# Sorting two row tiles in one instruction a stage, with ScalarE's copies of the idle ends made twice a merge

## What is computed

```python
def _L0_conv_ref(x):                       # x is normalised over its channels
    x3 = x.reshape(B, M, F)                # M = 4096 positions, F = 256
    corr = jnp.einsum('bmf,bnf->bmn', x3, x3) / F
    s = -jnp.sort(-corr, axis=-1)          # every row of 4096 sorted, largest first
    ranks = jnp.round(jnp.linspace(1.0, M - 1, NB_POOLS)).astype(jnp.int32)
    pooled = jnp.take(s, ranks, axis=-1)   # 256 of the 4096
    return pooled.reshape(B, H, W, NB_POOLS)
...
x = x + _L0_conv_ref(_ln_c(x))
t = _to_tokens(x)
t = t + _L0_ffn_ref(_ln_t(t), ...)         # experts, routed by attention over 1048576 edges
```

## Time and profile before

| | |
|---|---|
| median of three runs | 31163.97 us (31161.8 to 31172.99) |
| span of the profiled execution | 31832.6 us |
| `pool_rows`, first to last DVE instruction of the full stages | 4662 to 29096 us |
| DVE busy | 28357.2 us, 89% |
| PE busy | 25816.8 us, 81% |
| ACT busy | 22199.6 us, 70% |
| POOL busy | 15519.9 us, 49% |

### The profile page before, as it was taken

One profiled execution on the slowest core, in us unless ns is written; L12 is line 12 of the kernel. 1 busy time (PEld: TensorE's weight loads), 2 busy tenths in 40 slices (PEclk: granted clock), 3 DMA queues, 4 the chain that ended last, 5 costly groups with the idle time before them and its releaser, 6 DMA issues. The chain is left out here.

```text
span 31832.6 us, 519908 instructions
## 1 busy us (share of the span) xinstructions
PE 25816.8 (81%) x174835; PEld 11754.5 (37%) x175348; DVE 28357.2 (89%) x30738; ACT 22199.6 (70%) x34415; POOL 15519.9 (49%) x9076
## 2 busy tenths in 40 slices
PE   3888888888888888888888888888888888883474
PEld 3555533333333333333333333333333333332464
DVE  6888859999999999999999999989999999997435
ACT  1777777777777777777777777767777777774730
POOL 0000018888888888888888888887000000001510
PEclk8999999999999999999999999999999999996655
DMA  2000000000000000000000000000000000000103
GB/s 89 2 2 2 2 18 5 6 7 7 6 7 6 13 7 7 7 7 7 6 12 6 7 7 7 6 6 6 12 6 6 6 6 6 6 6 12 15 12 131
DMA packets 651302, 393.71 MB, mean 12 GB/s; under 512 B 425132, under 2 KB 604336, under 8 KB 646448
## 3 DMA queue, kind: packets, MB, share of 16 engines
q1 hardware_dynamic: 338034, 311.42, 3.1%
q0 software_dynamic: 290304, 22.40, 1.1%
q10 hardware_dynamic: 20288, 25.70, 0.2%
HBM read 196.49 MB, written 162.34 MB: 11 GB/s over the span
## 5 line engine op out<-in xcount | busy, mean ns | idle before, releaser
L1399 ACT ACTIVATE z<-psum 128x1024 f32<-128x1024 f32 x14208 | 14105.4, 1026 | 4046.7 <-PE psum L1157 2696.9
L1503 POOL DMA_INDIRECT sorted_d<-word_s,place_s x8192 | 14683.9, 1792 | 2643.7 <-issue 2476.9
L1157 PE MATMUL psum<-z,net 64*64 64x512 f32 x103424 | 13548.6, 619 | 2790.8 <-ACT z L1399 2536.0
L1357 DVE TENSOR_TENSOR arena<-arena 128x1536 f32<-128x1536 f32 (+17 forms) x6016 | 11654.5, 1937 | 1170.1 <-ACT arena L1438 637.6
L1358 DVE TENSOR_TENSOR arena<-arena 128x1536 f32<-128x1536 f32 (+17 forms) x6016 | 11647.7, 1936 | 0.0
L1157 PEld LDWEIGHTS psum<-z,net 64*64 64x64 f32 x103424 | 3128.9, 132 | 12044.9 <-issue 12018.0
L1673 POOL DMA_INDIRECT arena<-table_d,arena x752 | 762.1, 1013 | 7506.8 <-DVE arena L1597 7284.2
L1438 ACT ACTIVATE arena<-arena 128x2048 f32<-128x2048 f32 (+15 forms) x5248 | 3149.0, 600 | 466.9 <-DVE arena L1358 466.6
L978 ACT ACTIVATE arena<-cst,arena 128x128 bf16<-128x128 f32 x8320 | 2633.6, 389 | 608.9 <-PE psum L906 514.3
L1497 POOL DMA_DIRECT2D word_s<-words_d x64 | 37.6, 588 | 4798.8 <-issue 4663.0
L1164 PE MATMUL psum<-z,net 64*128 64x512 f32 x8192 | 1901.0, 601 | 208.4 <-ACT z L1399 199.9
(11 more groups left out here) (217 smaller groups left out, 18338.8 us busy)
## 6 DMA issues: line engine op xcount, KB each, us to landing
sorted_d<-word_s,place_s POOLq DMA_INDIRECT x8192
y_d<-ys SPq DMA_DIRECT2D x256, 256.0 KB
arena<-y_d SPq DMA_DIRECT2D x64, 1024.0 KB, 5.6
arena<-in_x SPq DMA_DIRECT2D x34, 512.0 KB, 5.1
x<-in_x SPq DMA_DIRECT2D x65, 256.0 KB
xnt_d<-arena SPq DMA_DIRECT2D x32, 512.0 KB, 3.1
hk_d<-arena SPq DMA_DIRECT2D x32, 512.0 KB, 4.3
arena<-hk_d SPq DMA_DIRECT2D x4, 4096.0 KB, 14.1
```

What stands on the lines that cost most here:

```text
L1157: last = nc.tensor.matmul(psum[n * HALF:(n + 1) * HALF, 2 * s + r, :], b.net[rr, at:at + HALF], flat[rr, n * BANK:(n + 1) * BANK], start=T ...
L1357: nc.vector.tensor_tensor(hi_out, hi_in, lo_in, ALU.max)
L1399: last = nc.scalar.activation(flat, bank, ACT.Abs)
L1503: pool.indirect_dma_start(out=b.sorted_d[:, :], out_offset=bass.IndirectOffsetOnAxis(ap=place_s[:, s, j:j + 1], axis=0), in_=word_s[:, s, ...
```

## The change

Both row tiles of a pair are now one operand. `half[n][g]` becomes `keys[n]`, 8192 keys wide; a full stage is one maximum and one minimum over both tiles (`compare`). Because the merge p = 128 leaves out the first 1024 keys of each tile, `fresh` is laid out as the high parts of both tiles, then the low parts of both, so that each is contiguous (`high`, `low`). Groups of up to 1024 keys stay whole in that layout; the stage (1024, 1024) reads the blocks from where they are and writes each tile in one piece again (`bring_together`, four instructions). Stage (256, 256) is four instructions too, as the low part comes from `fresh`.

The semaphores `sorted_` and `carried` are one each instead of one a tile. A stage waits for the one before it. ACT copies only twice a merge: `edges_of(p, 0)`, the keys from p/4 to p/2 of both ends of each group, and `edges_of(p, 1)`, the outer p/8 at both ends, both from the buffer that stage (p, p) wrote into the other one. DVE waits for the first at k = p/4 and for the second at k = p/16. In ACT's order they stand in the middle of the ticks of the stages k = p/2 and k = p/4. Nothing is changed in PE's, SP's and POOL's parts. The core of the diff:

```diff
+def edges_of(buf, p, which):
+    w, at, apart = ((p // 4, 1, 5), (p // 8, 0, 15))[which]
+    return buf.rearrange("p (n m w) -> p n m w", m=2 * p // w, w=w)[:, :, at::apart, :]
+def carried_before(s):
+    p, k = STAGES[s]
+    return 2 * MERGES.index(p) + (k <= p // 4) + (k <= p // 16)
...
             def sort(i, after_first):
...
-                    for g in range(2):
-                        if s == 0 and g == 0:
-                            for n in range(SLOTS):
-                                dve.wait_ge(fe_copied[n], (i + 1) * PER_PAIR)
-                        if s == 0 and after_first:
+                    source, target = keys[(s - 1) % 2], keys[s % 2]
+                    if s == 0:
+                        for n in range(SLOTS):
+                            dve.wait_ge(fe_copied[n], (i + 1) * PER_PAIR)
+                        if after_first:
                             dve.wait_ge(tailed, i * SPARSE)
-                        if s > 0 or after_first:
-                            dve.wait_ge(sorted_[g], i * N_FULL + s)
-                            dve.wait_ge(carried[g], i * N_CARRIED + kept_before(s))
-                        for source, from_, to in sources(s, g):
-                            hi_in, lo_in = compared(source[:, from_:to], p, k)
-                            hi_out, lo_out = compared(half[s % 2][g][:, from_:to], p, k)
-                            nc.vector.tensor_tensor(hi_out, hi_in, lo_in, ALU.max)
-                            last = nc.vector.tensor_tensor(lo_out, hi_in, lo_in, ALU.min)
-                        last.then_inc(sorted_[g], 1)
+                        last = compare(fresh[:, high], target[:, high], p, k)
+                    else:
+                        dve.wait_ge(sorted_, i * N_FULL + s)
+                        if k in (p // 4, p // 16):
+                            dve.wait_ge(carried, i * N_CARRIED + carried_before(s))
+                        if s < FIRST_MERGE:
+                            last = compare(source[:, high], target[:, high], p, k)
+                        elif s == FIRST_MERGE:
+                            compare(source[:, high], target[:, high], p, k)
+                            last = compare(fresh[:, low], target[:, low], p, k)
+                        elif (p, k) == (1024, 1024):
+                            last = bring_together(source, target)
+                        else:
+                            last = compare(source, target, p, k)
+                    last.then_inc(sorted_, 1)
...
-            def carry(i, s, g):
-                p, k = STAGES[s]
-                act.wait_ge(sorted_[g], i * N_FULL + s)
-                act.wait_ge(carried[g], i * N_CARRIED + kept_before(s))
-                first = LO if s < FIRST_MERGE else 0
-                nc.scalar.activation(carried_over(half[s % 2][g][:, first:M], p, k),
-                                     carried_over(half[(s - 1) % 2][g][:, first:M], p, k), ACT.Copy).then_inc(carried[g], 1)
+            def carry(i, p, which):
+                s = first_of(p)
+                act.wait_ge(sorted_, i * N_FULL + (s + 1))
+                to = 2 * (M - LO) if s < FIRST_MERGE else 2 * M
+                nc.scalar.activation(edges_of(keys[(s + 1) % 2][:, 0:to], p, which),
+                                     edges_of(keys[s % 2][:, 0:to], p, which), ACT.Copy).then_inc(carried, 1)
...
             def period(i, has_next, has_last):
                 for s, (p, k) in enumerate(STAGES):
                     ticks = ticks_of(s)
-                    for g in range(2):
-                        if k < p and s < N_FULL:
-                            carry(i, s, g)
-                        middle = len(ticks) // 2
-                        for tick in (ticks[middle:] if g else ticks[:middle]):
-                            if has_next:
-                                front(i + 1, tick)
-                            if has_last:
-                                ffn_piece(i - 1, tick)
+                    middle = len(ticks) // 2
+                    for tick in ticks[:middle]:
+                        if has_next:
+                            front(i + 1, tick)
+                        if has_last:
+                            ffn_piece(i - 1, tick)
+                    for which in range(2):
+                        if k == p >> (which + 1):
+                            carry(i, p, which)
+                    for tick in ticks[middle:]:
+                        if has_next:
+                            front(i + 1, tick)
+                        if has_last:
+                            ffn_piece(i - 1, tick)
```

More of the change, by code:

```diff
@@ L274 @@
 N_FULL = N_STAGES - SPARSE
-N_CARRIED = sum(k < p for p, k in STAGES[:N_FULL])
+MERGES = sorted({p for p, _ in STAGES})
+N_CARRIED = 2 * len(MERGES)
 FIRST_MERGE = sum(p == WIRES for p, _ in STAGES)
@@ L285, in compared, with first_of @@
     return m[:, :, :, 0, :], m[:, :, :, 1, :]
[L288 to L296, removed]
+def first_of(p):
+    return STAGES.index((p, p))
+def edges_of(buf, p, which):
[4 more added lines that the diff above has]
+    return 2 * MERGES.index(p) + (k <= p // 4) + (k <= p // 16)
 RANKS = [int(r) for r in np.round(np.linspace(1.0, M - 1, D))]
@@ L1011, in pool_rows @@
     sem, carve, psum, sb = b.sem, b.carve, b.psum, b.sb
-    half = [[b.arena[:, (2 * n + g) * M:(2 * n + g + 1) * M] for g in range(2)] for n in range(2)]
-    fresh = [b.arena[:, (4 + g) * M:(5 + g) * M] for g in range(2)]
-    fresh_v = b.arena[:, 4 * M:6 * M].rearrange("p (g m) -> p g m", g=2)
+    keys = [b.arena[:, 2 * n * M:2 * (n + 1) * M] for n in range(2)]
+    fresh = b.arena[:, 4 * M:6 * M]
+    fresh_low = fresh[:, 2 * (M - LO):].rearrange("p (g m) -> p g m", g=2)
+    fresh_high = fresh[:, 0:2 * (M - LO)].rearrange("p (g m) -> p g m", g=2)
     both = [b.arena[:, 2 * n * M:2 * (n + 1) * M].rearrange("p (g m) -> p g m", g=2) for n in range(2)]
@@ L1037, in pool_rows @@
     fe_copied = [sem(f"fe_copied{s}") for s in range(SLOTS)]
-    sorted_ = [sem(f"sorted{g}") for g in range(2)]
-    carried = [sem(f"carried{g}") for g in range(2)]
+    sorted_, carried = sem("sorted"), sem("carried")
     tailed = sem("tailed")
@@ L1310, in sparse @@
                 if s == N_FULL:
-                    for g in range(2):
-                        dve.wait_ge(sorted_[g], (i + 1) * N_FULL)
-                        dve.wait_ge(carried[g], i * N_CARRIED + kept_before(s))
+                    dve.wait_ge(sorted_, (i + 1) * N_FULL)
+                    dve.wait_ge(carried, (i + 1) * N_CARRIED)
                 else:
@@ L1327, in sparse, with compare, block_of, bring_together @@
                 last.then_inc(tailed, 1)
[L1329 to L1336, removed]
+            def compare(source, target, p, k):
+                hi_in, lo_in = compared(source, p, k)
+                hi_out, lo_out = compared(target, p, k)
+                nc.vector.tensor_tensor(hi_out, hi_in, lo_in, ALU.max)
+                return nc.vector.tensor_tensor(lo_out, hi_in, lo_in, ALU.min)
+            def block_of(buf, n):
+                n_high = (M - LO) // 1024
+                at, each = (n * 1024, M - LO) if n < n_high else (2 * (M - LO) + (n - n_high) * 1024, LO)
+                return bass.AP(buf.tensor, buf.offset + at, [buf.ap[0], [each, 2], [1, 1024]])
+            def bring_together(source, target):
+                for n in range(0, M // 1024, 2):
+                    hi_in, lo_in = block_of(source, n), block_of(source, n + 1)
+                    out = target.rearrange("p (g m) -> p g m", g=2)[:, :, n * 1024:(n + 2) * 1024]
+                    nc.vector.tensor_tensor(out[:, :, 0:1024], hi_in, lo_in, ALU.max)
+                    last = nc.vector.tensor_tensor(out[:, :, 1024:2048], hi_in, lo_in, ALU.min)
+                return last
             def sort(i, after_first):
+                high = slice(0, 2 * (M - LO))
+                low = slice(2 * (M - LO), 2 * M)
                 for s, (p, k) in enumerate(STAGES):
@@ L1390, in front @@
                         if tick + 1 == len(FRONT[0]) and s == 0 and not (isinstance(i, int) and i == 0):
-                            for g in range(2):
-                                act.wait_ge(sorted_[g], (i - 1) * N_FULL + FRESH_READ)
+                            act.wait_ge(sorted_, (i - 1) * N_FULL + FRESH_READ)
                         at = (j * SLOTS + s) * UNIT_GROUPS * WIRES
-                        last = nc.scalar.activation(fresh_v[:, :, at:at + UNIT_GROUPS * WIRES], bank, ACT.Copy,
+                        to, at = (fresh_low, at) if at < LO else (fresh_high, at - LO)
+                        last = nc.scalar.activation(to[:, :, at:at + UNIT_GROUPS * WIRES], bank, ACT.Copy,
                                                     bias=-1.0)
```

1 line of the change is left out of this document (removed).

## The result

| | before | after |
|---|---|---|
| median | 31162.89 us | 32739.29 us (32705.58 to 32747.31) |
| ratio | 1 | 1.0502, interval 1.0488 to 1.0517 |
| span of the profiled execution | 31832.6 us | 32740.6 us |
| DVE / ACT busy | 28357 / 22200 us | 28138 / 20630 us |
| POOL busy | 15520 us | 23681 us |

A forecast was written before the change was run, and what follows sets the result against it. DVE's sort bounds the kernel, with POOL's scatters hidden; after the change POOL ends last. 31164 before, plus 1310 for the longer stage and 200 for the profiler, gives 32674, say 32680 us; range about 32100 to 33250.

The forecast's parts named there:

- POOL takes its turns from DVE: In the sort, POOL gets one scatter through for each two-input DVE instruction, however long, each ending 0.92 us after a boundary.
- the first rival: POOL is not held beside the sort, so its scatters stay hidden: faster, likeliest 30,700 us; chance 0.11.
- 101 scatters a pair: Scatters fitting beside DVE's work after the change, where 128 are needed; 1730 left behind the sort, taking 2280 us.
- DVE's core: Sort time without idle: fewer instructions save 6.3 us a pair, new waits cost 5.9, leaving 367.9 us a pair.
- The waits for copies mostly go: DVE's waits in the sort for ScalarE's copies, 637.6 us over the stage, mostly vanish; bounds none to all.
- The coupling: Once POOL ends last, each microsecond DVE idles in the sort passes 0.79 scatter, worth 1.04 us behind it.
- The sum: First maximum to next phase: 23546 us sort, 2280 behind, 10 opening, 25836 against 24524 before, so +1310 us.
- the profiler: Extra DVE idle time beside POOL, some 385 us before the change; half, 200, was taken as only in the profiled execution.
- the opening of the next phase: Time after the last scatter until the next phase's first DVE instruction, put at 10 us.

The follow-up runs named there:

- split: The changed kernel with every comparison over both tiles cut into two instructions; 31354 us beside 31182 for the kernel before, ratio 1.0056.
- split_last: The changed kernel with only the eight full stages of the last merge (p = 2048) cut into two; 31850 us beside 33037 for the changed kernel.
- early_split_two: The changed kernel with copies at the head of their stages and the last two merges' full stages cut into two; 31343 us, ratio 0.9905 to the kernel before.
- one_input: The changed kernel with four extra one-operand DVE reductions a pair, their results unused; 33129 us beside 33067 for the changed kernel.
- copies_only: The kernel before with only the copies changed to twice a merge for each tile, row tiles staying apart; 30738 us beside 31182, ratio 0.9856.
- again: The kernel before, unchanged, run and profiled once more; 31184 us, span 31182.2 us.
- copies_second: The kernel before with only the copies changed to twice a merge, run a second time; 31073 us beside 31631, ratio 0.9822.
- joined_only: The kernel before with only the row tiles joined, copies still at every stage; 33597 us beside 33037 for the changed kernel.
- scatter_first: The changed kernel with POOL's scatters starting with the phase, without waiting for the first pair's front to be copied; 35225 us.

## Why the prediction was right, point by point

- **POOL takes its turns from DVE.** Right, and the deciding step. split gives the turns back and with them 1.4 ms; split_last and early_split_two lie between in order of their instructions (96, 112, 132 and 186 a pair: 6828, 7794, all and all scatters within the sort). one_input shows that DVE at work is not enough to hold a scatter: the maxima and minima do, a reduction of one operand does not. The two differ in their number of inputs, and also in what they write (as many elements as they read from each, or one), which no run tells apart. The section of the Trainium skill named with the first rival, SBUF — State Buffer, Who interferes with whom, says that a DVE instruction with two SBUF inputs contends with a GpSimd instruction that reads SBUF, and one with at most one such input, outside what it calls the 2-port perf modes, does not. The trace agrees: a scatter takes 4.15 us beside a maximum and 0.97 beside the reductions. The probe that the prediction quoted from the same section, in which tensor_tensor did not stall such DMAs, is not borne out here.
- **101 scatters a pair.** They were 106.7, just outside my bounds of 97 to 106. I took off 5 for boundaries that lie close together and for the pauses between batches, and added nothing for DVE's remaining idle time; the trace after has 8.0 us of it in each pair, of which 4.2 on average are one wait for a copy. So 1365 were left, not 1730, and 1798 us behind the sort, not 2280. How the 106.7 divide among boundaries and idle time was not counted.
- **DVE's core.** A pair takes 373.2 us with 8.0 idle; I had 367.9 without any. Across a stage the instructions start 0.10 us later than within (4.44 against 4.34), where I had 0.12. split, with the waits, takes 378.8 us a pair, copies_only 369.3; 3.7 of the difference are the late copy, and some 6 are left beside the 5.9 of the forecast. So 6.3 saved against 5.9 spent stands, within some 1 us a pair. The rule of the Trainium skill to minimise the count of operations and not of semaphores (VectorE: DVE Perf Modes, Rules for kernel authors), by which the waits would be free, does not stand here: the same two runs have nearly the same number of DVE instructions.
- **The waits for copies mostly go.** From 417.9 us (again) to 266.2, one large wait for each pair (4.89 us at 15240 in the trace): ScalarE reaches the copy for (512, 128) late. Half right; where tiles stay apart they go to 14.7 (copies_only) and 78.5 (copies_second).
- **The coupling.** Half right. Of 1.04 us back for each microsecond, one_input measured 442 of 504, or 0.88, for a pause in one piece, and joined_only 695 of 1221, or 0.57, for short ones. So the line that a wait which DVE loses or gains moves the end by nothing was too strong: such a wait costs a part of its length.
- **The sum.** From the first maximum to the next phase the changed kernel takes 30360.80 - 4660 = 25701 us, where I had 25836. The kernel before undisturbed takes 24148, where I had 24524 and gave 200 of the difference to the profiler. So both sides were too long, by 135 and by 176 us, and in the difference these nearly cancel. The 135 hide larger ones: the sort took 337 us more than forecast (23883, I had 23546, without idle time), the part behind it 482 less (1798, 2280), the opening of the next phase 10 more. These two are in part one error, as idle time lengthens the sort and lets scatters through: 510 us of it would give 403 scatters at 0.79 each (an estimate), and 365 more came. That the total was within 60 us is luck all the same; its larger terms by themselves were good to some 500.

The counterpart of one_input was not run: a filler with two inputs of the same length as the reductions, or one with a single input that writes as much as it reads.

## What to carry to other kernels

An engine that is off the path can be paced by the number of instructions of another: before making instructions longer, look in the timeline for an engine whose operations all end at a fixed offset from the other's starts, and count whether its work still fits. Where it does not, cut the long instructions, or put work that leaves the shared resource alone between them; in this kernel an instruction more, at 0.07 us, bought back 1.2 us while scatters were left behind the sort (split_last, 1187 us for 1024 instructions). And when a change has two halves, run each alone: here one gained 1.4 to 1.8% and the other lost 6%.

## What the runs showed of the hardware that was not expected

- **Long scatters only where DVE's stages follow without a wait.** The scatters by the line's own view, shortest, median and longest in ns, for again, copies_only, after and split in that order:

```profile
L1503 POOL DMA_INDIRECT sorted_d<-word_s,place_s x8192: 966/1830/62231, 4665.8 to 22857.9; - x200
```

```profile
L1512 POOL DMA_INDIRECT sorted_d<-word_s,place_s x8192: 966/1830/286887, 4680.1 to 22321.4; - x200
```

```profile
L1535 POOL DMA_INDIRECT sorted_d<-word_s,place_s x8192: 967/3061/9002, 4664.9 to 30339.6; - x200
```

```profile
L1540 POOL DMA_INDIRECT sorted_d<-word_s,place_s x8192: 966/1829/9002, 4674.3 to 21257.2; - x200
```

  In the kernels whose stages follow without a wait a scatter was held for up to 62 us (31 starts of DVE instructions) and 287 us (145 starts), and 12 to 28 of the 8192 took over 15 us. In all ten traces where each stage waits for the one before, none took over 9.03. Turns are lost in other places too: again had 169 scatters a pair and copies_only 171, with 188 sort instructions, and split 187 with 186. That a stage's wait always lets the scatter in, while a boundary without one can miss it (as one did in one_input), fits this and was not tested by itself.
- **Free scatters held up other engines.** 22 us at a time in scatter_first, 4222 us for a front of 360, with a scatter every 1.27 us. Beside the sort of split, with one in 2.03 us on average (16591 us for 8192), nothing of the kind lengthened it. That it is the slower pace which spares the other engines, and not something else about the first front, was not tested.
